# One head of four takes its row maximum over both key halves in one VectorE pass

## The reference, cut to what matters

```
q = jnp.einsum('bsc,hcd->bhsd', xn, wq)
k = jnp.einsum('btc,hcd->bhtd', yn, wk)
v = jnp.einsum('btc,hcd->bhtd', yn, wv)
a = jax.nn.softmax(jnp.einsum('bhsd,bhtd->bhst', q, k) * D ** (-0.5), axis=-1)
o = jnp.einsum('bhst,bhtd->bhsd', a, v)
```

## Time and profile before

| | |
|---|---|
| median of the runs | 1450.94 us |
| span of the profiled execution | 1480.6 us |
| PE busy | 1407.8 us, 95% of the span |
| DVE busy | 837.4 us, 57% |
| ACT busy | 762.4 us, 51% |
| POOL busy | 576.4 us, 39% |
| mean granted TensorE clock | 0.975 |
| main loop of `a2` with maxima (55 steps) | from about 1044 to 1216 us of the span |
| main loop of `a2` without maxima | from about 1218 to 1243 us |

### The profile page before, as it was taken

How to read it: one execution, slowest core, us unless ns; L and a number is a source line. 1 busy time by engine, 2 the same in 40 slices (tenths; PEclk the granted TensorE clock), 3 DMA queues, 4 the chain that set the end, 5 groups by cost and what they waited for, 6 DMA issues and landing times.

```text
span 1480.6 us, 24805 instructions
## 1 busy us (share of the span) xinstructions
PE 1407.8 (95%) x9880; PEld 807.5 (55%) x9880; DVE 837.4 (57%) x1739; ACT 762.4 (51%) x1161; POOL 576.4 (39%) x629
## 2 busy tenths in 40 slices
PE   8999999999999988899999999998999999997997
PEld 5677853333333256787653433753344445667996
DVE  3288547669999464126763774346788882222221
ACT  4544225656666645233254777332688885323331
POOL 3053134233334333521021565501688886405111
PEclk9999999999999999899999999997799999998999
DMA  7000000000110048562300002404000001833100
GB/s 226 1 1 1 1 12 1 15 8 16 44 40 19 3 152 297 195 220 68 33 23 0 10 24 79 130 0 135 1 10 16 9 16 38 330 118 102 34 17 10
DMA packets 81810, 90.85 MB, mean 61 GB/s; under 512 B 31969, under 2 KB 65726, under 8 KB 80543
## 3 DMA queue, kind: packets, MB, share of 16 engines
q1 hardware_dynamic: 78782, 83.01, 18.2%
q0 software_dynamic: 2912, 6.26, 1.2%
HBM read 67.92 MB, written 21.48 MB: 60 GB/s over the span
## 4 chain that ended last, share of the span: by engine, by line
PE 85%; DVE 9%; issue 2%; ACT 2%; POOL 1%; another core or an unknown queue 1%; DMA 0%; POOLq 0%; DVEq 0%; ACTq 0%
PE psum L1717 12%; PE psum L1736 10%; PE psum L1675 6%; PE psum L4140 6%; PE psum L736 4%; PE psum L3392 4%; PE psum L3383 4%; PE psum L1933 4%; PE psum L1759 3%; PE psum L4151 3%; PE psum L2863 2%; DVE a_nm L1846 2%; PE psum L2869 2%; PE psum L3361 2%; PE psum L724 2%
## 5 line engine op out<-in xcount | busy, mean ns | idle before, releaser
L1846 DVE TENSOR_REDUCE a_nm<-psum 128x1 f32<-128x512 f32 x302 | 199.6, 686 | 99.8 <-PE psum L1675 97.3
L1846 DVE TENSOR_REDUCE xa_nm<-psum 128x1 f32<-128x512 f32 x256 | 161.8, 683 | 49.6 <-PE psum L1675 44.0
L1771 ACT ACTIVATE xn<-psum 128x1024 f32<-128x1024 f32 (+1 forms) x96 | 86.2, 949 | 52.0 <-PE psum L1717 52.0
L1771 ACT ACTIVATE a_w<-psum 128x1024 f32<-128x1024 f32 x86 | 83.4, 1021 | 17.8 <-PE psum L1717 17.3
L1717 PE MATMUL psum<-a2qT,a2kT 32*128 32x512 f32 x512 | 90.3, 608 | 0.0
L1771 ACT ACTIVATE xa_w<-psum 128x1024 f32<-128x1024 f32 (+2 forms) x96 | 79.7, 885 | 19.6 <-PE psum L1717 19.4
L1675 PE MATMUL psum<-a2kr,a2qr 32*128 32x512 bf16 x256 | 71.5, 408 | 6.4 <-DVE a_nm L1846 5.7
L1707 PE MATMUL psum<-a_mrow,onesb 2*128 2x512 bf16 x384 | 69.2, 392 | 0.3 <-DVE a_mrow L1875 0.2
L1675 PE MATMUL psum<-xa_ckr,xa_cqr 32*128 32x512 bf16 x256 | 65.7, 382 | 1.7 <-POOL xa_ckr L1980 1.0
L1675 PEld LDWEIGHTS psum<-a2kr,a2qr 32*128 32x128 bf16 x256 | 20.8, 92 | 76.0 <-DVE a_nm L1846 49.2
L670 POOL TENSOR_SCALAR pf_kdd<-pf_kdd 128x1024 f32<-128x1024 f32 x8 | 22.2, 2775 | 97.2 <-ACT pf_kdd L841 97.2
(11 more groups left out here) (591 smaller groups left out, 3488.4 us busy)
## 6 DMA issues: line engine op xcount, KB each, us to landing
mo_w<-in_L_ffn_W SPq DMA_DIRECT2D x14, 1024.0 KB
sw_wv<-in_L_ffn_w_v SPq DMA_DIRECT2D x4, 2048.0 KB, 18.9
scratch_a2v<-co_stages SPq DMA_DIRECT2D x16, 256.0 KB
scratch_a2k<-co_stages SPq DMA_DIRECT2D x16, 256.0 KB
a2kT<-scratch_a2k SPq DMA_DIRECT2D x8, 512.0 KB, 7.8
a2v<-scratch_a2v SPq DMA_DIRECT2D x4, 1024.0 KB, 11.7
sw_wp<-in_L_ffn_w_proj SPq DMA_DIRECT2D x4, 1024.0 KB, 19.6
a_raw<-scratch_a_dens SPq DMA_DIRECT2D x56, 64.0 KB, 2.1
```

The lines of the kernel that those rows point to most:

```text
L1771: e.activation(self.weights(n, c)[:, 2 * jj:2 * jj + 2, lo:S], ps[:, pr:pr + 2, lo:S], ACT.Exp, scale=self.scale).then_inc(*self.weighed.m ...
L1846: e.tensor_reduce(self.nm[n % 3][:, q, part, h:h + 1], view, AX.X, ALU.max, negate=True).then_inc(*self.max_taken.mark(*i))
```

## The change

For head 3 alone, and for `a2` alone (`paired = (3,)`), the two halves are joined. GpSimd prepares the keys so that, for head 3, the first half holds the difference (first half minus second half). The product of part 0 is then the excess of one half over the other; ScalarE copies it with Relu to SBUF ("keep"). The product of part 1 is the plain one of the second half. One `tensor_tensor_reduce` of VectorE adds the kept excess to it, which gives the larger of both halves in each column, and takes its (negated) maximum along the row. So of the eight products for a chunk of 128 queries, seven are taken by VectorE and one by ScalarE. Before, VectorE took all eight, two of them from ScalarE's copies.

`Pace` places the products anew: `pair_kept` takes the excess if it is among the next four, else a product of head 2 or a second half of head 3 whose excess was kept; `behind_rows` takes one more of the latter kinds; `pair_behind` takes two of heads 0 and 1 as before. The same rules run in the lead-in, where ScalarE now has to run the "keep" steps too. Two tiles serve as early copies there. The three `nm` tiles are filled once by GpSimd, as the column of head 3's first half is no longer written.

```diff
     def pair_kept(self, n):
-        if self.fits(n, "rows"):
+        if self.a.paired:
+            step = self.among(n, self.a.is_excess) or self.among(n, self.is_upper)
+            if step:
+                yield from self.place(step)
+        elif self.fits(n, "rows"):
             yield from self.keep(self.chosen((2, 3)))
+    def among(self, n, kind):
+        return next((step for step in self.maxima_left()[:4] if kind(step[1])), None) if self.fits(n, "rows") else None
+    def is_upper(self, item):
+        return item[3] > 1 and (item in self.outstanding if self.a.is_lower(item) else not self.a.is_excess(item))
     def behind_rows(self, n, c):
-        if self.held and self.fits(n, "rows"):
+        if self.a.paired:
+            step = self.among(n, self.is_upper)
+            if step:
+                yield from self.place(step)
+        elif self.held and self.fits(n, "rows"):
             yield from self.place(self.chosen((2, 3)))
         yield from self.held_taken()
     def pair_behind(self, n):
         for count in range(2):
-            if self.fits(n, "rows"):
+            if self.a.paired:
+                step = self.among(n, lambda item: item[3] < 2)
+                if step:
+                    yield from self.place(step)
+            elif self.fits(n, "rows"):
                 yield from self.place(self.chosen((0, 1)))
...
+    def is_excess(self, item):
+        return item[3] in self.paired and item[2] == 0 and self.jobs[item[0]].mode == "full"
+    def is_lower(self, item):
+        return item[3] in self.paired and item[2] == 1 and self.jobs[item[0]].mode == "full"
...
+        for t in self.nm if self.paired else ():
+            w.wait_ge(*pool.now())
+            e.memset(t[:, :, :, :], -NEG).then_inc(*self.set.mark("halves"))
...
-                e.activation(kept[:, :], ps[:, self.pair_of("max", *i), :], ACT.Copy).then_inc(*self.max_kept.mark(*i))
+                e.activation(kept[:, :], ps[:, self.pair_of("max", *i), :], ACT.Relu if self.paired else ACT.Copy).then_inc(*self.max_kept.mark(*i))
...
+                elif self.is_lower(i):
+                    w.wait_ge(*self.max_kept.at(*self.excess_of(i)))
+                    kept, _ = self.kept_at(self.excess_of(i))
+                    e.tensor_tensor_reduce(out=kept[:, :], in0=view, in1=kept[:, :], scale=-1.0, scalar=-NEG, op0=ALU.add, op1=ALU.min,
+                                           accum_out=self.nm[n % 3][:, q, part, h:h + 1]).then_inc(*self.max_taken.mark(*i))
...
-            e.tensor_copy(self.kr[b][:, g, :], self.kT[:, g, b * keys:(b + 1) * keys]).then_inc(*self.rounded.mark(b, g))
+            kr, first, early, late = self.kr[b][:, g, :], 32 * self.attention.paired[0], slice(b * keys, b * keys + S), slice(b * keys + S, (b + 1) * keys)
+            e.tensor_copy(kr[:, S:keys], self.kT[:, g, late]).then_inc(*self.rounded.mark(b, g, "late"))
+            w.wait_ge(*self.k.pool.now())
+            e.tensor_copy(kr[0:first, 0:S], self.kT[0:first, g, early]).then_inc(*self.rounded.mark(b, g, "early"))
+            w.wait_ge(*self.k.pool.now())
+            e.tensor_tensor(kr[first:P, 0:S], self.kT[first:P, g, early], self.kT[first:P, g, late], ALU.subtract).then_inc(*self.rounded.mark(b, g))
```

More of the change, by code:

```diff
@@ L1045, in __init__ @@
         self.ahead = 3 if self.folded else 2
-        self.held = None
+        self.held, self.outstanding = None, {attention.taker(item): 0.0 for item in attention.kept_items if ("max", attention.taker(item)) in self.left}
+        attention.early = len(attention.kept_items)
     def begin(self, mode, groups=range(4), after=0.0):
@@ L1096, in place @@
     def place(self, step):
+        if self.a.is_excess(step[1]):
+            yield from self.keep(step)
+            return
         job = self.jobs[step[1][0]]
@@ L1104, in place @@
         self.occupy(time, groups)
-        self.take(step, self.now + time, self.TAKE)
+        self.take(step, max(self.now + time, self.outstanding.pop(step[1], 0.0)), self.TAKE)
         yield step
@@ L1126, in keep @@
         self.banks[bank] = self.scalar + self.HELD - self.TAKE
-        self.held = step[1], self.scalar
+        if self.a.paired:
+            self.outstanding[self.a.taker(step[1])] = self.scalar
+        else:
+            self.held = step[1], self.scalar
         self.a.keep_next(step[1])
@@ L1284, in __init__ @@
     def __init__(self, k, tag, owner, jobs, d, scale, mem, upper=False, causal=False, weights=(), outs=(), group=1):
-        self.group, self.folded, self.kept = group, d < 32, []
+        self.group, self.folded, self.kept, self.paired = group, d < 32, [], ()
         self.k, self.tag, self.owner, self.jobs, self.d, self.scale, self.upper = k, tag, owner, jobs, d, scale, upper
@@ L1314, in __init__, with keep_maxima @@
         self.weighed, self.raw_copied, self.den_copied = (k.by_scalar(tag + n) for n in ("_weighed", "_raw_copied", "_den_copied"))
-    def keep_maxima(self, mem):
+    def keep_maxima(self, mem, paired=(), early=()):
+        self.paired = paired
         self.kept = [self.k.sb(f"{self.tag}_kept{i}", [P, S], F32, mem) for i in range(2)]
+        self.kept_early = early or self.kept
         self.max_kept = self.k.by_scalar(self.tag + "_max_kept")
@@ L1327, in kept_at, with taker, excess_of @@
         i = self.kept_items.index(item)
-        return self.kept[i % 2], self.kept_items[i - 2] if i > 1 else None
+        tiles = self.kept_early if i < self.early else self.kept
+        return tiles[i % 2], self.taker(self.kept_items[i - 2]) if i > 1 else None
+    def is_excess(self, item):
+        return item[3] in self.paired and item[2] == 0 and self.jobs[item[0]].mode == "full"
+    def is_lower(self, item):
+        return item[3] in self.paired and item[2] == 1 and self.jobs[item[0]].mode == "full"
+    def taker(self, item):
+        n, i, part, h = item
+        return (n, i, 1, h) if self.paired else item
+    def excess_of(self, item):
+        n, i, part, h = item
+        return n, i, 0, h
     def keep_outs(self, outs):
@@ L1358, in items, with paired_items @@
             return [(n, i, j, 0) for i in range(SC) for j in range(i + 1)]
+        if len(self.paired) == 2:
+            return [item for t in range(2 * SC + 1) for item in self.paired_items(n, t)]
         return [(n, i, half, h) for i in range(SC) for half in range(self.halves(n)) for h in (2, 0, 3, 1)]
+    def paired_items(self, n, t):
+        i, half = divmod(t, 2)
+        excess, plain = [(n, i, 0, 2 + half)], [(n, i, half, 0), (n, i, half, 1)]
+        lower = [(n, i, 1, 2) if half else (n, i - 1, 1, 3)]
+        return (excess if t < 2 * SC else []) + (lower if t else []) + (plain if t < 2 * SC else [])
     def maxima(self):
@@ L1376, in start @@
         self.coming, self.given, self.bank_of, self.kept_items = list(self.maxima()), 0, {}, []
+        self.early = 2 * len(self.coming)
     def give(self, count):
@@ L1383, in give @@
             count -= step[0] != "max_parts"
-            yield step
+            if step[0] == "max" and self.is_excess(step[1]):
+                self.keep_next(step[1])
+                yield "keep", step[1]
+            else:
+                yield step
     def left_until_rows(self, n):
@@ L1839, in vector_steps @@
                     w.wait_ge(*(self.max_taken.at(n - 3, "all") if self.folded else self.max_parts.at(n - 3, 1)))
+                if self.paired:
+                    w.wait_ge(*self.set.at("halves"))
                 view = ps[:, self.pair_of("max", *i), :]
@@ L3143, in __init__ @@
                             lambda n: [self.xturn.form_copied(f, n, 1) for f in range(FC)], self.kT, self.kr)
-                self.attention.keep_maxima(att)
+                self.attention.keep_maxima(att, (3,) if cross else (), self.attention.dens_kept)
                 for b in range(B):
@@ L3422, in scalar_program @@
                 e.activation(self.v[:, i, :], ps[:, banks.of(self.pre + "_v", i), :], ACT.Copy).then_inc(*self.value_copied.mark(self.pre, i))
+            else:
+                self.attention.scalar_steps(e, w, [(step, i)])
         self.attention.scalar_steps(e, w, self.attention.order())
```

## The result

The changed kernel takes 1468.29 us (median of 11 runs, 1461.62 to 1471.62), the kernel before 1451.96 in the runs beside it. The ratio is 1.0111, with a 95% interval of 1.0094 to 1.0128: slower by 16 us, between 13.6 and 18.6. I had forecast 1463.7, with a range of 1451 to 1471.

The account below looks back on a forecast made before the run. Values wait for the last maximum product, which waits for VectorE to empty a bank. Loop +10.8 and fused operation +2.2 give +13.0 on the span, +12.7 on the median: 1450.9 to 1463.7 us, range 1451 to 1471.

Parts of the forecast that it names:

- Order of the steps: Main loop of a2: two step types alternate, 28 without an excess to copy and 27 with one.
- Step A: Main-loop step without ScalarE's copy: VectorE empties two banks one after the other before the values, 3.52 us.
- Step B: Main-loop step where ScalarE copies the excess beside a VectorE reduction: 2.97 us, as on the path now.
- Loop: 55 steps of a2's main loop: 181.9 us against 171.1, +10.8; +13.0 with the fused operation's surcharge.
- Fused operation: VectorE's joined add and maximum in 28 steps: 0.08 us more than a reduction each, +2.2 us in all.
- Transposes: Step that turns a job's maxima: denominators start 0.44 us later than usual, 7 times, 3.1 us kept.
- ScalarE, keys: Fewer ScalarE copies free 17 us but gain nothing; GpSimd's key preparation, at most 14.4 us against 4.62, costs nothing.
- Lead-in: Before the main loop, five ScalarE copies replace reductions: -3 to +3 us, taken as 0.
- Rival 1: Faster: VectorE's own loop was the limit in the main loop, -4.1 us, 1447 us; chance 0.14.
- Rival 2: No change: steps behind long ones catch up the lost time in the main loop, +0.9 us, 1452; chance 0.06.
- Rivals 3 and 4: Fused operation at half speed, +27.6 us, 1478; or Relu reloads ScalarE's tables, +69 us, about 1530; chance together 0.04.

Follow-up runs that it names:

- e4: Changed kernel with a plain reduction in place of the fused operation: 1466.04 us, ratio 1.0079, +10.6 us to the kernel before at equal clock.
- e2: Changed kernel with heads 2 and 3 both paired, products listed in another order: 1461.10 us, ratio 1.0049, +2.4 us to the kernel before at equal clock.
- e3: Changed kernel with ScalarE's plain copy of head 2 put back in steps without an excess: 1457.32 us, ratio 1.0014, +1.3 us at equal clock.
- e8: Changed kernel with GpSimd's key preparation as before, one cast for each job: 1468.99 us, ratio 1.0105, +10.9 us to the kernel before at equal clock.
- e10: The changed kernel run again, nothing altered: 1468.10 us, ratio 1.0084, mean clock 0.9851.
- e9: Changed kernel with the lead-in of a2 as before the change and plain keys for job 0: 1459.68 us, ratio 1.0049, mean clock 0.9901.
- e5: Changed kernel with heads 2 and 3 both paired and the transposes ahead of the denominators: 1461.27 us, ratio 1.0054, -0.7 us at equal clock.

## Why the prediction was right

- *Order of the steps*: A and B alternate, as read from `Pace`.
- *Step A*: 3.52 predicted, 3.52 to 3.53 measured, by the path that the sum names: in the timeline of the step at 1097.54 its terms are 1.43, 0.42, 0.62, 0.69, 0.05 and 0.32, where I had 1.43, 0.43, 0.60, 0.69, 0.06 and 0.31. *Step B*: 2.97 and 2.96 to 3.02. The cause I gave for B is only half right: the changed kernel's chain there goes through the scores, and VectorE's release of M4's bank comes at the same time. Both lengths agree by luck, so the sum didn't suffer.
- *Loop*: from the first score (1031.18) to the last product of a maximum (1212.64) 181.5 us, against 170.4 before (1044.78 to 1215.13), +11.1. Both begin at the lower clock; by the jobs at full clock, 1.63 us in 8 steps, it is 11.2 for 55 steps. Predicted +13.0, of which 10.8 without the fused operation's surcharge.
- *Fused operation*: predicted +0.08 in 28 steps; the next reduction starts 0.62 behind it (1105.88 to 1106.50 in the timeline) against 0.60, so 0.02, and e4 gives 0.6 us. The surcharge of 2.2 us is the term that I had too large. The trace agrees with the Trainium skill's rule (VectorE: DVE Perf Modes, section "Two Vector instructions with no wait between them") that such an operation is two instructions. That the read of 83 ns costs a slot of its own, which was my upper estimate, does not hold: it starts together with the next reduction.
- *Transposes*: I kept them at 0.44 a job, between values and denominators. They moved behind the denominators, which I did not see. In the changed kernel this costs little more (3.87 is 0.35 above a step A, and the step behind it is 0.15 longer, 0.50 in all), because step A is long anyway. In e2 and e3 it used up 3.1 and 2.2 us at equal clock.
- *ScalarE, keys*: no gain from ScalarE's 28 fewer copies, nothing for the keys (e8). Relu: 600 ns, and one table load as with Copy.
- *Lead-in*: I took 0 +- 3; at equal clock it is 1.3 (e10 less e9). The parts don't add up quite: with the loop's 11.2 that would be 12.5, and the whole is 11.2 +- 0.6.
- *The clock*: I had no term for it. It is 4.3 us of the difference between the medians, from a lead-in that more often runs at the lower level.

The median is 1468.3 and not 1463.7 for these reasons: the clock (+4.3), an equal-clock difference of 11.2 where I had 12.7 (-1.5), a kernel before of 1451.96 in the runs beside it where I had 1450.94 (+1.0), and 0.8 that the line doesn't explain. The mechanism and the size of the loop's loss were right by their own terms. That the median still lies within my range is luck in part, since the room above it was meant for a dearer fused operation and not for the clock.

Rival 1 (VectorE's loop as the limit) falls: VectorE's share of a job fell from 84% to 71%, and the job grew. Rival 2 falls, since steps B keep 2.97. Rivals 3 and 4 fall by the rows of the new operations.

## What to carry to other kernels

An engine that only copies out of PSUM may look like waste, since the copy is read once more; here it was the second exit of a ring of two banks, and taking it away cost 0.55 us in every second step although VectorE's and ScalarE's busy times fell. Before trading one engine's work for another's, count for each bank who empties it, and follow the product that stands ahead of the next large one. And where a planner decides by estimates, look after a change at what else it has moved: the place of the transposes was worth 2 to 3 us at equal clock, and with the late place no paired kernel came below the one before.

## What the runs showed of the hardware

- One kernel's runs differ by over 15 us, and the differences go with the granted clock of TensorE: 0.96 us for each 0.001 of its mean over the run. The clock's mean depends on the kernel (0.979 for e5, 0.990 for e9), so a median of raw times mixes two effects, and a change in one short stage can move the mean of all.
- VectorE's `tensor_tensor_reduce` with an accumulated output on 128x512 fp32, one operand in PSUM and one in SBUF, takes 690 ns, as a plain reduction does (686). The read of the accumulator overlaps with the operation behind it.
